# The last attention: weights mixed through differences, and two steps moved on VectorE

## What is computed

```python
pooled = hidden_states.mean(axis=1)
logits = jax.nn.relu(pooled @ Wg1 + bg1) @ Wg2 + bg2
vals, idx = jax.lax.top_k(logits, TOP_K)          # TOP_K = 2, four experts
sm = jax.nn.softmax(vals, axis=-1)
weights = jnp.zeros_like(logits).at[jnp.arange(B)[:, None], idx].set(sm)
def moe_proj(W, b):
    Wc = jnp.einsum('be,ecd->bcd', weights, W)
    return jnp.einsum('btc,bcd->btd', hidden_states, Wc) + (weights @ b)[:, None, :]
...
scores = jnp.einsum('bthd,bshd->bhts', q, k) / np.sqrt(D)
attn = jax.nn.softmax(scores, axis=-1)
out = jnp.einsum('bhts,bshd->bthd', attn, v).reshape(B, T, C)
return out @ Wo + bo
```

## Time and profile before

| what | value |
|---|---|
| median of 3 runs | 2086.02 us (2083.6 to 2088.55) |
| profiled execution, its own time | 2087.51 us |
| its span | 2085.8 us |
| TensorE, VectorE, ScalarE, GpSimd busy | 88%, 78%, 63%, 55% of the span |
| the last attention | 1783 to 2085 us of the span |

### The profile page before, as it was taken

One profiled execution on the slowest core, in us unless ns is written; L12 is line 12 of the kernel. 1 busy time (PEld: TensorE's weight loads), 2 busy tenths in 40 slices (PEclk: granted clock), 3 DMA queues, 4 the chain that ended last, 5 costly groups with the idle time before them and its releaser, 6 DMA issues. The chain is left out here.

```text
span 2085.8 us, 80049 instructions
## 1 busy us (share of the span) xinstructions
PE 1837.7 (88%) x31023; PEld 1449.2 (69%) x31023; DVE 1635.5 (78%) x3978; ACT 1310.4 (63%) x3796; POOL 1154.4 (55%) x1556
## 2 busy tenths in 40 slices
PE   5999977989999969999989986999877663899998
PEld 4777754667888858888867763777766452677776
DVE  6988877867888868888856667676655897799998
ACT  4667674655666646666545545555544683699997
POOL 6777754875555435555568863744554275233332
PEclk9999997999999989999999997999998786799999
DMA  5222212001222156000011110135552530000000
GB/s 127 54 53 53 52 37 61 1 20 55 83 72 69 39 83 31 1 1 1 1 27 41 40 29 23 44 134 167 190 201 79 150 100 17 2 19 19 19 19 24
DMA packets 185355, 116.73 MB, mean 56 GB/s; under 512 B 82556, under 2 KB 177432, under 8 KB 181272
## 3 DMA queue, kind: packets, MB, share of 16 engines
q1 hardware_dynamic: 173656, 74.27, 15.0%
q0 software_dynamic: 8064, 35.97, 4.9%
q10 hardware_dynamic: 3264, 1.38, 0.3%
HBM read 83.28 MB, written 28.27 MB: 53 GB/s over the span
## 5 line engine op out<-in xcount | busy, mean ns | idle before, releaser
L1621 POOL TENSOR_TENSOR L1f_hl<-L1f_h,L1f_hh 128x512 fp32r<-128x512 f32 x128 | 167.2, 1307 | 125.7 <-DVE L1f_hh L1633 125.3
L1580 ACT ACTIVATE L1f_h<-L1f_H,L1f_w_b 128x512 f32<-128x512 f32 x192 | 132.4, 690 | 100.9 <-PE L1f_H L1033 94.4
L412 POOL TENSOR_TENSOR L3f_wide<-L3f_flat,head_of_row 128x512 f32<-128x512 f32 x64 | 66.8, 1043 | 190.0 <-PE L3f_S L487 168.8
L1633 DVE CAST L1f_hh<-L1f_h 128x512 fp32r<-128x512 f32 x192 | 126.0, 663 | 33.4 <-ACT L1f_h L1580 31.5
L2006 DVE TENSOR_TENSOR L2f_both_h<-L2f_both_G,L2f_both_act 128x512 f32<-128x512 f32 x114 | 78.6, 690 | 91.5 <-ACT L2f_both_act L1981 67.7
L1981 ACT ACTIVATE L2f_both_act<-L2f_both_A 128x512 f32<-128x512 f32 x114 | 68.2, 598 | 120.2 <-PE L2f_both_G L1033 78.9
L1898 POOL DMA_INDIRECT token_y<-L1f_w_w,L2f_both_token x88 | 89.7, 1019 | 76.1 <-DVE L1f_w_w L2025 53.5
L412 POOL TENSOR_TENSOR L1a_wide<-L1a_flat,head_of_row 128x512 f32<-128x512 f32 x64 | 66.5, 1040 | 112.8 <-ACT L1a_flat L695 112.8
L719 DVE TENSOR_REDUCE L1a_mx<-L1a_S 128x16 f32<-128x1024 f32 x64 | 78.4, 1225 | 56.8 <-PE L1a_S L487 56.8
L621 ACT ACTIVATE L1a_probs_T<-L1a_PT 128x512 f32<-128x512 f32 x64 | 38.2, 597 | 95.6 <-PE L1a_PT L451 95.6
L1425 ACT ACTIVATE L0f_parts<-L0f_psA,L0f_w_logits 128x128 f32<-128x128 f32 x256 | 73.0, 368 | 37.6 <-PE L0f_psA L1484 37.6
(11 more groups left out here) (560 smaller groups left out, 6879.3 us busy)
## 6 DMA issues: line engine op xcount, KB each, us to landing
L0a_mask_raw<-mask SPq DMA_DIRECT2D x256, 32.0 KB, 2.0
expert_split<-L1a_split_halves SPq DMA_DIRECT2D x7, 1152.0 KB, 6.0
L2f_both_xhat<-sorted_x SPq DMA_DIRECT2D x22, 258.0 KB
sorted_x<-L1f_zero SPq DMA_DIRECT2D x4, 1408.0 KB, 22.2
L0a_ctxT<-ctx_T SPq DMA_DIRECT2D x64, 64.0 KB, 1.9
L1a_ctxT<-ctx_T SPq DMA_DIRECT2D x64, 64.0 KB, 1.9
L1a_mask_raw<-mask SPq DMA_DIRECT2D x256, 0.1 KB
L2a_ctxT<-ctx_T SPq DMA_DIRECT2D x64, 64.0 KB, 2.1
```

The costliest lines, as they stand in the source:

```text
L412: pool.tensor_tensor(wide[:, s], flat[:, s, :].rearrange("p (b n) -> p b n", b=B2).unsqueeze(2).broadcast_to([P, B2, 4, S]), c.head_of_row ...
L1580: act.activation(h[:, q % 3, :], psH[:, q % 2, :], ACT.Relu, bias=b1[:, q:q + 1]).then_inc(h_kept, 1)
L1621: pool.tensor_tensor(hl[:, q % 3, :], h[:, q % 3, :], hh[:, q % 3, :], ALU.subtract).then_inc(hl_pool, 1)
L1633: dve.tensor_copy(hh[:, q % 3, :], h[:, q % 3, :]).then_inc(hh_made, 1)
```

## The change

Three things change in the last attention.

The weights are mixed through differences. With a softmax over two experts the two weights add up to one, so the mixture is w_first x (W_first - W_last) + W_last. Six tables of differences are made once, on GpSimd, in the block of the gates; `at` now holds the offset of the pair in that table and the offset of the last expert. The two scalings on ScalarE and their register load are gone, and VectorE reads both offsets, with two register loads.

The subtraction of the maxima is one instruction of 1024 columns in place of two of 512.

The order changes. On ScalarE xhat stands ahead of the second exponential, and the copy to `xT` goes from VectorE to ScalarE. On VectorE the register loads, the subtraction and the mixing stand behind the sum into x.

```diff
@@ ScalarE, step
-                if moe:
-                    for u, s in at(i, r, 0):
-                        _, first_at = nc.values_load_multi_w_load_instructions(...)
...
-                        act.activation(Wa[:, s, 0, :], w_all[:, bass.ds(first_at[0], 3 * P)], ACT.Copy,
-                                       scale=moe["two"][:, 0, bass.ds(B2 * u, 1)])
...
+                for u, s in at(i, r, 1):
+                    wait(act, xT_done, u + 1)
+                    wait(act, v_done if moe else qk_done, u - 3)
+                    act.activation(xT[:, s, :], psTY[:, 0:P], ACT.Copy).then_inc(xT_kept, 1)
...
@@ VectorE, step: taken out between mx and rden
-                        wait(dve, xT_done, u + 1)
-                        wait(dve, v_done, u - 3)
-                        dve.tensor_copy(xT[:, s, :], psTY[:, 0:P]).then_inc(xT_kept, 1)
...
@@ VectorE, step: behind the sum into x
+                if moe:
+                    for u, s in at(i, r, 1):
+                        _, pair_at = nc.values_load_multi_w_load_instructions(
+                            moe["at"][0:1, 0, bass.ds(B2 * u, B2)], engines=(mybir.EngineType.DVE,),
...
+                        _, last_at = nc.values_load_multi_w_load_instructions(
+                            moe["at"][0:1, 1, bass.ds(B2 * u, B2)], engines=(mybir.EngineType.DVE,),
...
+                for u, s in at(i, r, 4):
+                    wait(dve, max_made, u + 1)
+                    wait(dve, pt1_done, u - 1)
...
+                    if moe:
+                        dve.tensor_tensor(less[:, s % 2].rearrange("p (g j) k -> p g j k", j=4), S4,
+                                          mx4.unsqueeze(3).broadcast_to([P, 4, 4, S]), ALU.subtract
+                                          ).then_inc(less_made, 2)
+                        continue
...
+                            last = dve.scalar_tensor_tensor(
+                                out=Wc[:, s, b, :], in0=w_less[:, bass.ds(pair_at[b], 3 * P)],
+                                scalar=moe["two"][:, bass.ds(B2 * u + b, 1)],
+                                in1=w_all[:, bass.ds(last_at[b], 3 * P)], op0=ALU.mult, op1=ALU.add)
+                        last.then_inc(wc_made, 1)
@@ mixture_gates, GpSimd
+            for l in range(1, E):
+                for f in range(l):
+                    pool.tensor_tensor(moe["less"][:, l * (l - 1) // 2 + f, :],
+                                       w_all[:, f, :, :].rearrange("p j n -> p (j n)"),
+                                       w_all[:, l, :, :].rearrange("p j n -> p (j n)"), ALU.subtract
+                                       ).then_inc(less_made, 1)
```

More of the change, by code:

```diff
@@ L26 @@
 APART = -(2.0 ** 120)
-IN_RANGE = "at most four places of 384 columns, added up from products of 0 or 1 with 0, 384, 768 and 1152"
+IN_RANGE = "at most six places of 384 columns, added up from products of 0 or 1 with multiples of 384"
 def wait(eng, sem, n, last=None):
@@ L695, in step @@
                         act.activation(kd[:, s, :], psQKV[:, P:2 * P], ACT.Copy).then_inc(qk_kept, 1)
-                if moe:
-                    for u, s in at(i, r, 0):
-                        act.activation(Wa[:, s, 1, :], w_all[:, bass.ds(first_at[1], 3 * P)], ACT.Copy,
-                                       scale=moe["two"][:, 0, bass.ds(B2 * u + 1, 1)]).then_inc(wa_made, 1)
+                for u, s in at(i, r, 0) if moe else ():
+                    wait(act, xT_done, u - 3)
+                    act.activation(xhat[:, s, :], c.x[:, u, :], ACT.Identity, bias=c.nmr[:, bass.ds(u, 1)],
+                                   scale=c.rstd[:, bass.ds(u, 1)]).then_inc(xhat_made, 1)
                 for u, s in at(i, r, 5):
@@ L703, in step @@
                                    ).then_inc(pt1_kept, 1)
-                for u, s in at(i, r, 0) if moe else ():
-                    wait(act, xT_done, u - 3)
-                    act.activation(xhat[:, s, :], c.x[:, u, :], ACT.Identity, bias=c.nmr[:, bass.ds(u, 1)],
-                                   scale=c.rstd[:, bass.ds(u, 1)]).then_inc(xhat_made, 1)
             run_steps(act, NT, DEPTH, RING, step)
@@ L2419, in mixture_gates @@
         sem = lambda n: sems(f"{name}_{n}")
[L2420 to L2421 removed]
+        mean_of, every, mean_rstd, earlier, place, pairs = (moe[n] for n in ("mean_of", "every", "mean_rstd",
+                                                                              "earlier", "place", "pairs"))
         K4 = NT // 4
@@ L2469, in _ @@
             run(dve.tensor_reduce(first[:, :], at[:, :], AX.X, ALU.add))
-            dve.tensor_tensor(first[:, :], first[:, :], last[:, :], ALU.subtract).then_inc(at_made, 1)
+            run(dve.tensor_tensor(first[:, :], first[:, :], last[:, :], ALU.subtract))
+            run(dve.tensor_tensor(at[:, :], rank[:, :], pairs[:, :], ALU.mult))
+            run(dve.tensor_reduce(pair_no[:, :], at[:, :], AX.X, ALU.max))
+            dve.tensor_tensor(pair_no[:, :], pair_no[:, :], first[:, :], ALU.add).then_inc(at_made, 1)
             dve.wait_ge(at_made, 1)
@@ L2477, in _ @@
             dve.wait_ge(w_made, 1)
-            for j, where in enumerate((first, last)):
-                run(dve.scalar_tensor_tensor(out=part[:, :], in0=place[:, :], scalar=where[:, 0:1], in1=w[:, :],
-                                             op0=ALU.is_equal, op1=ALU.mult))
-                run(dve.tensor_reduce(two[:, j:j + 1], part[:, :], AX.X, ALU.add))
-            dve.tensor_copy(two[:, :], two[:, :]).then_inc(two_made, 1)
+            run(dve.scalar_tensor_tensor(out=part[:, :], in0=place[:, :], scalar=first[:, 0:1], in1=w[:, :],
+                                         op0=ALU.is_equal, op1=ALU.mult))
+            dve.tensor_reduce(two[:, :], part[:, :], AX.X, ALU.add).then_inc(two_made, 1)
             dve.wait_ge(at_spread, 1)
@@ L2485, in _ @@
             dve.wait_ge(two_spread, 1)
-            run(dve.tensor_copy(moe["two"][:, :, :].rearrange("p j b -> p (j b)"), psP[:, 0:2 * NB]))
+            run(dve.tensor_copy(moe["two"][:, :], psP[:, 0:NB]))
             dve.wait_ge(pe_done, 3)
@@ L2511, in _ @@
             pe.wait_ge(at_made, 1)
-            for j, where in enumerate((first, last)):
+            for j, where in enumerate((pair_no, last)):
                 mm = pe.matmul(psA[:, j * NB:(j + 1) * NB], where[:, 0:1].broadcast_to([NB, P]), c.ident[0:NB, 0:NB],
@@ L2516, in _ @@
             pe.wait_ge(two_made, 1)
-            for j in range(2):
-                mm = pe.matmul(psP[:, j * NB:(j + 1) * NB], two[:, j:j + 1].broadcast_to([NB, P]),
-                               c.ident[0:NB, 0:NB], start=True, stop=True, skip_group_check=True)
-            mm.then_inc(two_spread, 1)
+            pe.matmul(psP[:, 0:NB], two[:, 0:1].broadcast_to([NB, P]), c.ident[0:NB, 0:NB], start=True, stop=True,
+                      skip_group_check=True).then_inc(two_spread, 1)
             pe.wait_ge(w_made, 1)
```

78 lines of the change are left out of this document (32 added, 46 removed).

## The result

| | median | runs |
|---|---|---|
| before, on the same chip | 2087.28 us | 4, 2083.60 to 2089.74 |
| changed | 2412.00 us | 4, 2402.02 to 2415.39 |

The ratio is 1.1531, with a 95% interval of 1.1504 to 1.1558. The change costs 324.7 us. The prediction was 2178 us, +92, in a range to 2195: right in direction, wrong in size by a factor of 3.5.

The account below looks back on a forecast made before the run. Three full engines were taken to bound the last attention at 4.41 us a step; a ring of 6.01 would replace it: 354.4 us against 260.3, +94.1, with +1.2 and -3 +92.3, so 2178 us, range 2138 to 2195.

Parts of the forecast that it names:

- The scope: Only the last attention was read and costed, from 1783 us to the end of the span.
- 1, the ring: Last attention: S, TensorE's work to O and Y, rden, On, sum, subtraction, next S form one chain of 6.01 us a step.
- 2, the loads: Two register loads of 0.527 us between sum and subtraction lie exposed; the subtraction starts at 4.68 us, not 3.71.
- the rival's sum: Step of the last attention if both register loads are hidden: 3.71 + 1.22 + 0.11 = 5.04 us; chance 0.08.
- The rival of hidden loads: VectorE's two register loads run early or overlap the sum: a step of 5.04 us, 2121 us; chance 0.08.
- 3, one subtraction of 1024 columns: On VectorE it takes 1.22 us, like the reduction over the same columns, and ends at 5.90 us of the step.
- 4, the mixing: VectorE's two mixings, 1.06 us to the next start, run beside TensorE's work and cost nothing, 0.35 us to spare.
- 5, ScalarE: Its work drops from 4.41 to some 3.4 us a step, a gain worth nothing behind the first steps.
- 6 and the sum: Stage ends, +1.2 and -3 us, added to +94.1 from the steps: +92.3 us, 2178 us.
- The start, put at -3: Start of the last attention: earlier xhat and QK and lighter gates save 3 us, between 0 and 5.
- the rival with 0.06: TensorE's clock falls to 1.2 GHz because it idles 1.9 us a step: 2200 us and more; chance 0.06.

Follow-up runs that it names:

- a1: Changed kernel with the subtraction back right behind mx in the first and second attention (L0a, L1a) only; 2258.37 us, ratio 1.079.
- a4: Changed kernel plus 20 useless matmuls on TensorE ahead of S in each of steps 8 to 64 of the last attention; 2342.91 us, ratio 1.124.
- a3: Changed kernel with both register loads moved up right behind mx, subtraction and mixing left behind the sum; 2287.76 us, ratio 1.098.
- b3: Kernel before with only one subtraction of 1024 columns in place of two of 512 in the last attention; 2080.18 us, ratio 0.999.
- a2: Changed kernel with the subtraction right behind mx in all three attentions, loads and mixing left behind the sum; 2137.43 us, ratio 1.024.
- b1: Changed kernel with loads, subtraction and mixing all back behind mx, ahead of rden, On and the sum; 2113.95 us, ratio 1.014.
- c1: b1 with xhat on ScalarE back behind the second exponential, as in the kernel before; 2082.69 us, ratio 1.002.
- b2: Changed kernel with loads and subtraction back right behind mx, only the mixing behind the sum; 2105.94 us, ratio 1.011.

## Why the prediction was right or wrong

- **The scope: wrong, 152 us.** The step that failed stands ahead of all terms: "The last attention starts at 1783 us and runs to the end" was the only stage read. The moved block serves three attentions, in front of the reader in the diff's indentation, and the order of instructions was compared in one. In L0a and L1a the same ring closes without loads or mixing, and costs 1.2 us a step more than the order before. Shown by a1.
- **1, the ring: right.** In the step at 2.4 GHz, counted from the start of S: O ends at 3.00 us (2.97 predicted), Y at 3.43 (3.39), rden starts at 3.05 (3.02), the sum at 3.56 (3.51), the subtraction at 4.73 (4.68), the next S at 6.05 (6.01). a4, with the clock held, has 6.07 on average.
- **2, the loads: right.** The first starts at 2211.89, just when Y's end (2211.85) frees the sum's wait, and they follow one another: 2211.89 to 2213.00, 1.11 us for 1.08. a3 without them has a step of 5.07, where the rival's sum had 5.04. The rival of hidden loads is dead. The Trainium skill, "Advanced Engine Details and Errata", section "Sequencer Loop", speaks of an instruction that waits for its semaphores in the queue. The changed kernel doesn't decide on that, since the sequencer has a separate wait (L37, 0.02 us long) at 2211.8, ahead of the loads; only the load behind the held-up mx speaks against running early. The floor of about 600 ns for such a load in the Trainium skill, "DMA: Bandwidth & Descriptors", section "Latency and other measured facts", isn't seen: the medians are 534 and 535 ns.
- **3, one subtraction of 1024 columns: right.** 1.22 us. b3 shows that by itself it is worth nothing that can be measured.
- **4, the mixing: right where it stands, incomplete.** It cost nothing in the changed kernel. That it is free only under the longer ring (a2), and stretched as soon as `wide` runs beside it (b1, c1), the text didn't see.
- **5, ScalarE: right.** Its work fell (51.91 us of 100 in the window above) and gained nothing. The earlier xhat is harmless here, and costs 26 us in the order of b1.
- **6 and the sum: short by some 12 us.** +92.3 was the sum for the last attention; a4 shows +104.5 from first to last mx. From mx of tile 2 to mx of tile 61 a4 took 364.2 us, for the 354.4 of the sum: 2.5 us because the median step was 6.05, and 7.3 in steps that were longer, one of 9.25 at the low clock and others of 6.1 to 6.7, whose cause was not followed. The start, put at -3, gave next to nothing: the last row maximum of L3a to the first mx took 62.5 us before and 62.3 in the changed kernel, and the first two steps 0.4 us less.
- **The clock: the rival with 0.06 came true, 59 us.** The text had both numbers, TensorE busy for 4.1 us in a step of 6 and idle for 1.9, and dismissed them with one stretch of 10 us in a stage with another pattern, beside a stage of some 380 us of this one. The rival's size was low too: 2200 and more, from "a fifth of the steps hit at over 1.5 us each", which is some 18 us where 59 were measured. Here 80 us ran wholly at 1.2 GHz, at 8.6 us a step, and the granted clock was 0.86 to 0.88 behind that. This loss feeds itself: the stretch from S to O is on the ring, so half the clock makes it 2.2 us longer. Shown by a4, and by a3 from the other side.

Together: 151.9 (scope) + 104.5 (ring) + 59.2 (clock) + 8.2 (not told apart from variation) = 323.8, the difference of the spans. With the ring sized rightly, the forecast failed by two steps: it costed the order in one attention of three, and it put the clock at nothing.

## What to carry to other kernels

Before costing a move in a function with a flag, list every stage that calls it, and compare the order in each: a block outside the `if` moves everywhere. When an engine's order puts a release (here of S's banks) behind a wait for a later product of the engine that needs the release, add up the ring from rows; that sum held to 0.05 us a step here. Then look at what the new idle time does to TensorE's clock before calling it done, for the price of idling can be half as much again as the ring itself.

## What the runs showed of the hardware

- **Useless matmuls made the kernel faster.** In a ring that leaves TensorE idle for 1.80 us of a 6.05 us step at 2.4 GHz, its granted clock was 0.50 for 80 us, in which it was busy for 69.7 and the gap was 1.15 us a step, and 0.86 to 0.88 later. With the gap filled to 0.59 us it was 1.00 from 2000 us on, and the stage took 59 us less. L0a and L1a, busy for 261 of 326 us and 296 of 350, kept 1.00 as well.
- **VectorE's mixing and GpSimd's additions took turns.** Two mixings took 1.14 us alone, 1.98 in b1, where `wide` (1.04 us) starts behind the first, and 1.78 in b2, where it starts ahead of it. GpSimd's bias addition took 0.77 us for 0.45. The ends alternate: in b2 `wide` 1954.51, first mixing 1954.92, bias addition 1955.24, second mixing 1955.65; in b1 `wide` 1960.37, second mixing 1960.78, bias addition 1961.09. The reduction mx, with one input and that in PSUM, kept 1.22 beside the same `wide`. The Trainium skill, "SBUF — State Buffer", section "SBUF: two separate sides", says that VectorE instructions with two SBUF inputs and GpSimd's share a port pair as an exclusive lock, held for a whole instruction. The trace agrees: each of the three mixings that waited here ends 0.41 us after GpSimd's instruction does.
- **A register load takes 0.53 us of VectorE's sequencer, and two didn't overlap** (1.11 us for both). One hides under a 1.2 us instruction (the kernel before); two and the waits behind them don't quite, and left some 0.5 us in 13 of 45 steps (c1).
